# Two floors and two reciprocals of the quantised feed-forward taken together on two columns

## The reference, cut to what matters

```python
def _act_quant(x):
    scale = 127.0 / jnp.clip(jnp.max(jnp.abs(x), axis=-1, keepdims=True), 1e-05)
    xq = jnp.clip(jnp.round(x * scale), -128.0, 127.0) / scale
    return x + jax.lax.stop_gradient(xq - x)

def _bitlinear(x, w):
    return jnp.einsum('bsi,oi->bso', _act_quant(x), _weight_quant(w))
gate = jax.nn.silu(_bitlinear(x, w_gate))      # 256 -> 1024
up = _bitlinear(x, w_up)                       # 256 -> 1024
return _bitlinear(gate * up, w_down)           # 1024 -> 256
```

## Time and profile before

| | before |
|---|---|
| median of 3 runs | 1256.86 us (1255.3 to 1258.94) |
| the profiled execution | 1257.31 us, span of the core 1255.5 us |
| busy over the span | PE 94%, PEld 75%, DVE 65%, ACT 51%, POOL 45% |
| VectorE work of the feed-forward (first `am` to last `sc`) | 384.2 to 480.0 us of the span |
| small VectorE operations touched | 32 floors (TENSOR_SCALAR, 154 ns each) and 32 reciprocals (164 ns each) |
| wide ones beside them | `am` over 1024 values 1220 ns, `am` over 256 values 420 ns, 16 of each |
| granted TensorE clock | full in every slice of the span |

### The profile page before, as it was taken

One profiled execution on the slowest core, in us unless ns is written; L12 is line 12 of the kernel. 1 busy time (PEld: TensorE's weight loads), 2 busy tenths in 40 slices (PEclk: granted clock), 3 DMA queues, 4 the chain that ended last, 5 costly groups with the idle time before them and its releaser, 6 DMA issues.

```text
span 1255.5 us, 30244 instructions
## 1 busy us (share of the span) xinstructions
PE 1184.3 (94%) x9760; PEld 936.2 (75%) x9760; DVE 819.8 (65%) x1805; ACT 643.1 (51%) x1394; POOL 559.1 (45%) x833
## 2 busy tenths in 40 slices
PE   6899999989998878989998999999999999999998
PEld 4688888767775446767776888888888888888886
DVE  4688888867776888868999774444444544444444
ACT  4776677645454887535556434434343343433332
POOL 2244444657774444558885323333333233333232
PEclk9999999999999999999999999999999999999999
DMA  8200000000001001200000233333333333333331
GB/s 278 69 24 17 17 17 8 2 2 1 0 0 34 1 1 42 61 26 2 0 0 21 75 113 110 116 117 104 103 114 117 124 115 117 104 105 112 117 104 63
DMA packets 34041, 80.13 MB, mean 64 GB/s; under 512 B 4416, under 2 KB 12096, under 8 KB 33984
## 3 DMA queue, kind: packets, MB, share of 16 engines
q1 hardware_dynamic: 32800, 78.09, 19.1%
q10 hardware_dynamic: 1184, 1.31, 0.3%
HBM read 77.03 MB, written 2.36 MB: 63 GB/s over the span
## 4 chain that ended last, share of the span: by engine, by line
PE 78%; DVE 8%; issue 5%; POOL 4%; ACT 3%; DMA 0%; DVEq 0%; POOLq 0%; ACTq 0%; SPq 0%
PE ps L2443 10%; PE ps L2441 10%; PE ps L2442 10%; PE ps L444 5%; PE ps L2523 5%; PE ps L2524 5%; PE ps L2525 5%; PE ps L1095 4%; PE ps L459 3%; PE ps L432 3%; PE ps L1086 2%; PE ps L1074 2%; PE ps L1102 2%; PE ps L1065 2%; POOL Sm L1406 2%
## 5 line engine op out<-in xcount | busy, mean ns | idle before, releaser
L2810 POOL TENSOR_TENSOR sw<-sg,wb 128x512 f32<-128x512 f32 x136 | 176.4, 1297 | 386.7 <-ACT sg L2634 352.8
L2713 DVE TENSOR_TENSOR a<-sw,ps 128x512 f32<-128x512 f32 x136 | 93.4, 687 | 224.8 <-POOL sw L2810 224.5
L2639 ACT ACTIVATE ah<-a 128x512 fp32r<-128x512 f32 x136 | 86.0, 632 | 290.7 <-DVE a L2713 268.4
L2441 PE MATMUL ps<-Hh,wh 128*128 128x512 f32 x544 | 215.3, 396 | 0.0
L2442 PE MATMUL ps<-Hl,wh 128*128 128x512 f32 x544 | 214.4, 394 | 0.0
L2443 PE MATMUL ps<-Hh,wl 128*128 128x512 f32 x544 | 214.4, 394 | 0.0
L2717 DVE TENSOR_TENSOR al<-a,ah 128x512 fp32r<-128x512 f32 x136 | 95.6, 703 | 62.4 <-ACT ah L2639 59.3
L760 ACT ACTIVATE Pr<-ps,mx 128x256 f32<-128x256 f32 x256 | 104.1, 479 | 61.2 <-DVE mx L629 56.6
L2443 PEld LDWEIGHTS ps<-Hh,wl 128*128 128x128 f32 x544 | 101.8, 187 | 25.1
L2441 PEld LDWEIGHTS ps<-Hh,wh 128*128 128x128 f32 x544 | 101.9, 187 | 24.8 <-issue 0.8
L2442 PEld LDWEIGHTS ps<-Hl,wh 128*128 128x128 f32 x544 | 101.9, 187 | 23.5
(11 more groups left out here) (238 smaller groups left out, 2459.7 us busy)
## 6 DMA issues: line engine op xcount, KB each, us to landing
wb<-token_weights SPq DMA_DIRECT2D x64, 512.0 KB, 3.6
raw<-in_ew SPq DMA_DIRECT2D x66, 384.0 KB, 3.0
cT<-in_ctxT SPq DMA_DIRECT2D x16, 256.0 KB, 2.7
cx<-in_ctxT SPq DMA_DIRECT2D x15, 256.0 KB, 2.8
X<-in_x SPq DMA_DIRECT2D x1, 1536.0 KB, 7.1
wqkv<-in_wqkv SPq DMA_DIRECT2D x2, 768.0 KB, 5.1
raw3g<-in_wg SPq DMA_DIRECT2D x1, 1024.0 KB, 5.4
raw3u<-in_wu SPq DMA_DIRECT2D x1, 1024.0 KB, 7.6
```

Source lines behind the costliest of these rows:

```text
L2441: eng.matmul(ps[:, bank, :], wh[:, u, w], HhT[:, c, cols], start=(c == 0), stop=False)
L2713: eng.tensor_tensor(a[:, tt, :], sw[:, tt, :], ps[:, UB[tt], :], ALU.mult).then_inc(m_a, 1)
L2810: eng.tensor_tensor(sw[:, tt, :], sg[:, tt, :], wb[:, u, tt * UT:(tt + 1) * UT], ALU.mult).then_inc(m_sw, 1)
```

## The change

`am`, `ac` and `sc` get two columns for each buffer: column 0 for the inner values of tile i, column 1 for the row of tile i+2. Both maxima are taken first, and one floor and one reciprocal then work on both columns (`scale_both`). The two opening tiles have only column 1, and the last two steps only column 0. The readers take their column, and `round2` and `scale2` wait on the semaphores `f_sc` and `f_ac` of the joint operations (two of the semaphores go). `scale_both` carries the waits that protect both columns.

```diff
@@ -1492,8 +1492,8 @@
     L = 2
     base = NPAIR * L
 
-    am = sb("am3", [P, 2, 1]); ac = sb("ac3", [P, 2, 1]); sc = sb("sc3", [P, 2, 1]); dq = sb("dq3", [P, 2, 3])
-    am2 = sb("am32", [P, 2, 1]); ac2 = sb("ac32", [P, 2, 1]); sc2 = sb("sc32", [P, 2, 1]); dq2 = sb("dq32", [P, 2, 1])
+    am = sb("am3", [P, 2, 2]); ac = sb("ac3", [P, 2, 2]); sc = sb("sc3", [P, 2, 2])
+    dq = sb("dq3", [P, 2, 3]); dq2 = sb("dq32", [P, 2, 1])
     r = sb("r3", [P, 2, DIM]); xqT = sb("xqT3", [P, 2, HALF, P], BF16)
     sg = sb("sg3", [P, 2, INNER]); a = sb("a3", [P, 2, INNER]); ar = sb("ar3", [P, 2, INNER])
     aqT = sb("aqT3", [P, 2, 8, P], BF16); y = sb("y3", [P, 2, DIM])
@@ -1504,7 +1504,7 @@
     f_am = sem(n + "am"); f_ac = sem(n + "ac"); f_sc = sem(n + "sc"); f_dq = sem(n + "dq")
     f_r = sem(n + "r"); f_xt = sem(n + "xt"); f_xte = sem(n + "xte")
     f_g = sem(n + "g"); f_u = sem(n + "u"); f_sg = sem(n + "sg"); f_a = sem(n + "a")
-    f_am2 = sem(n + "am2"); f_ac2 = sem(n + "ac2"); f_sc2 = sem(n + "sc2"); f_dq2 = sem(n + "dq2")
+    f_am2 = sem(n + "am2"); f_dq2 = sem(n + "dq2")
     f_ar = sem(n + "ar"); f_at = sem(n + "at"); f_ate = sem(n + "ate"); f_o = sem(n + "o"); f_y = sem(n + "y")
     f_rnd = sem(n + "rnd")
     g["f_sg"] = f_sg; g["f_a"] = f_a; g["f_xte"] = f_xte; g["f_ate"] = f_ate; g["f_y"] = f_y
@@ -1628,16 +1628,30 @@
         eng.memset(rnd[:, 0:1], ROUND).then_inc(f_rnd, 1)
         eng.memset(rnd[:, 1:2], -ROUND).then_inc(f_rnd, 1)
 
-        def front1(i, u):
+        def row_max(i, u):
             eng.wait_ge(ln_h, base + i + 1)
-            eng.tensor_reduce(am[:, u, :], h[:, u, :], AX.X, ALU.max,
+            eng.tensor_reduce(am[:, u, 1:2], h[:, u, :], AX.X, ALU.max,
                               apply_absolute_value=True).then_inc(f_am, 1)
-            eng.wait_ge(f_am, i + 1)
-            reach(eng, f_dq, i - 1)
-
-            eng.tensor_scalar(ac[:, u, :], am[:, u, :], 1e-5, 1.0 / 127.0, ALU.max, ALU.mult).then_inc(f_ac, 1)
-            eng.wait_ge(f_ac, i + 1)
-            eng.reciprocal(sc[:, u, :], ac[:, u, :]).then_inc(f_sc, 1)
+
+        def inner_max(i, u):
+            eng.wait_ge(f_a, 2 * i + 2)
+            eng.tensor_reduce(am[:, u, 0:1], a[:, u, :], AX.X, ALU.max,
+                              apply_absolute_value=True).then_inc(f_am2, 1)
+
+        def scale_both(i, u):
+
+
+            c = slice(0 if within(i, 0, last) else 1, 2 if within(i, -2, last - 2) else 1)
+            if within(i, -2, last - 2):
+                eng.wait_ge(f_am, i + 3)
+            reach(eng, f_am2, i + 1)
+            reach(eng, f_dq, i + 1)
+            reach(eng, f_dq2, i - 1)
+            eng.tensor_scalar(ac[:, u, c], am[:, u, c], 1e-5, 1.0 / 127.0, ALU.max, ALU.mult).then_inc(f_ac, 1)
+            eng.wait_ge(f_ac, i + 3)
+            reach(eng, f_ar, i - 1)
+            reach(eng, f_r, i + 1)
+            eng.reciprocal(sc[:, u, c], ac[:, u, c]).then_inc(f_sc, 1)
 
         def mul(i, u, q):
             eng.wait_ge(f_sg, 2 * i + q + 1)
@@ -1648,22 +1662,12 @@
                                      scalar=dq[:, u, 1:2], in1=sg[:, u, q * 512:(q + 1) * 512],
                                      op0=ALU.mult, op1=ALU.mult).then_inc(f_a, 1)
 
-        def amax2(i, u):
-            eng.wait_ge(f_a, 2 * i + 2)
-            eng.tensor_reduce(am2[:, u, :], a[:, u, :], AX.X, ALU.max,
-                              apply_absolute_value=True).then_inc(f_am2, 1)
-            eng.wait_ge(f_am2, i + 1)
-            reach(eng, f_dq2, i - 1)
-            eng.tensor_scalar(ac2[:, u, :], am2[:, u, :], 1e-5, 1.0 / 127.0, ALU.max, ALU.mult).then_inc(f_ac2, 1)
-            eng.wait_ge(f_ac2, i + 1)
-            eng.reciprocal(sc2[:, u, :], ac2[:, u, :]).then_inc(f_sc2, 1)
-
         def body(i, u):
             v = 1 - u
             if within(i, 0, last):
                 mul(i, u, 0)
                 mul(i, u, 1)
-                amax2(i, u)
+                inner_max(i, u)
             if within(i, -1, last - 2):
                 reach(eng, f_r, i + 1)
                 ln_dve2(eng, L, i + 2, u, f_r)
@@ -1671,7 +1675,9 @@
                 eng.wait_ge(f_r, i + 1)
                 ln_dve2(eng, L + 1, 0, u, f_r)
             if within(i, -2, last - 2):
-                front1(i + 2, u)
+                row_max(i + 2, u)
+            if within(i, -2, last):
+                scale_both(i, u)
             if within(i, -2, last - 3):
                 ln_dve(eng, L, i + 3, v)
             elif isinstance(i, int) and i == last - 2:
@@ -1679,11 +1685,13 @@
 
         def first():
 
-            front1(0, 0)
+            row_max(0, 0)
+            scale_both(-2, 0)
             ln_dve(eng, L, 1, 1)
             yield PART
             ln_dve2(eng, L, 1, 1, f_r)
-            front1(1, 1)
+            row_max(1, 1)
+            scale_both(-1, 1)
             ln_dve(eng, L, 2, 0)
 
         yield from pairs(eng, body, first)
@@ -1700,10 +1708,10 @@
                            scale=dq[:, u, 0:1]).then_inc(f_sg, 1)
 
         def round2(i, u):
-            eng.wait_ge(f_sc2, i + 1)
+            eng.wait_ge(f_sc, i + 3)
             reach(eng, f_at, i - 1)
             eng.activation(ar[:, u, :], a[:, u, :], ACT.Identity, bias=rnd[:, 0:1],
-                           scale=sc2[:, u, :]).then_inc(f_ar, 1)
+                           scale=sc[:, u, 0:1]).then_inc(f_ar, 1)
 
         def xt_out(i, u):
             eng.wait_ge(f_xt, i + 1)
@@ -1758,18 +1766,18 @@
             eng.wait_ge(f_sc, i + 1)
             reach(eng, f_xt, i - 1)
             eng.nop(nofuse=True)
-            eng.tensor_scalar(r[:, u, :], h[:, u, :], sc[:, u, :], ROUND, ALU.mult, ALU.add).then_inc(f_r, 1)
+            eng.tensor_scalar(r[:, u, :], h[:, u, :], sc[:, u, 1:2], ROUND, ALU.mult, ALU.add).then_inc(f_r, 1)
 
         def scales(i, u):
             reach(eng, f_sg, 2 * (i - 1))
             reach(eng, f_a, 2 * (i - 1))
             eng.nop(nofuse=True)
-            eng.tensor_scalar(dq[:, u, :], wsc[:, :], ac[:, u, :], None, ALU.mult).then_inc(f_dq, 1)
+            eng.tensor_scalar(dq[:, u, :], wsc[:, :], ac[:, u, 1:2], None, ALU.mult).then_inc(f_dq, 1)
 
         def scale2(i, u):
-            eng.wait_ge(f_ac2, i + 1)
+            eng.wait_ge(f_ac, i + 3)
             reach(eng, f_y, i - 1)
-            eng.tensor_tensor(dq2[:, u, :], wsc[:, 2:3], ac2[:, u, :], ALU.mult).then_inc(f_dq2, 1)
+            eng.tensor_tensor(dq2[:, u, :], wsc[:, 2:3], ac[:, u, 0:1], ALU.mult).then_inc(f_dq2, 1)
 
         def add_x(t, u):
             eng.wait_ge(f_y, t + 1)
```

## The result

| | before | changed |
|---|---|---|
| median of 12 runs | 1256.72 us (1255.3 to 1258.94) | 1252.45 us (1251.83 to 1253.96) |
| profiled execution, span | 1255.5 us | 1251.2 us |
| VectorE instructions recorded | 1805 | 1777 |

The ratio is 0.9965 with a 95% interval of [0.9957, 0.9973]: 4.3 us, 0.35%, faster. The forecast was 1252.4 us.

What follows compares the result with a forecast made beforehand. VectorE was taken to bound the feed-forward loop at 5.34 us a tile; with ScalarE's 4.85 us taking over, 62.71 us becomes 58.06, 4.65 us earlier: 1252.7 us from the profiled 1257.31, stated as 1252.4 us median, range 1250.6 to 1256.2.

Steps and rivals of the forecast that it cites:

- VectorE sets the pace before: Feed-forward loop: VectorE bounds it at 5.34 us a tile, 10.67 us a turn, including 0.47 us idle at the turn back.
- Without the pair `h` starts 1.14 us after the wide maximum: VectorE: without floor and reciprocal before `h`, it starts after 1.14 us, not 1.67 and 1.53, saving 0.92 us a turn.
- ScalarE and TensorE then set the pace at 4.85 us a tile: Loop after the change: ScalarE with TensorE needs 3.72 + 1.13 = 4.85 us a tile and becomes the limit.
- the sum: From fourth to last `xqT`: ten steps at 4.85 and two at 4.78 make 58.06 instead of 62.71 us, 4.65 us earlier.
- VectorE's turn of 9.75 us, and a lead that loses at most 0.3 us: Loop: VectorE's turn falls from 10.67 to 9.75 us; it enters 0.8 us ahead and loses at most 0.3 us altogether.
- Rival B: VectorE's saving not had in full, or given back behind the layer: gain 0 to 3.5 us, 1255 us in the middle; chance 0.17.
- The second column costs under 0.01 us: Joint floor and reciprocal on VectorE: one column more in each was worth under 0.01 us, taken as nothing.
- The added waits cost nothing: VectorE: the joint floor's four semaphore waits and the joint reciprocal's three were taken as costing nothing.
- Rival C: Added waits worked off one by one behind the row's maximum: at 0.2 us each, 4.8 us slower, 1261.6 us; chance 0.06.
- rival A: TensorE's jump at the loop's turn back shows once `r` is early: gain only 3.1 us, 1254.0 us; chance 0.15.
- Both semaphores on the inner scale: Inner reciprocal moved later: would end at 435.70, just before `ar` at 435.72, with VectorE's 0.8 us lead on top; no cost.
- The gain passes to the end: Behind this layer everything waits in turn and DMA has 0% of the chain, so the whole 4.65 us reaches the end.

Runs made afterwards that it cites:

- 1: Kernel before with the wide maximum taken over 512 of the 1024 inner values: 1251.61 us, ratio 0.9956.
- 3: Kernel before with the five turns of the feed-forward's loop written out: 1251.03 us, ratio 0.9953.
- 2: Changed kernel with the wide maximum taken over 512 of the 1024 inner values: 1252.65 us, ratio 0.9955.
- 7: Changed kernel with four no-operation instructions on VectorE ahead of the feed-forward's first work: 1252.27 us, ratio 0.9965.
- 9: Changed kernel with two no-operation instructions ahead on VectorE: 1251.69 us in a single execution.
- 10: Changed kernel with one no-operation instruction ahead on VectorE: 1253.07 us in a single execution.
- 11: Changed kernel with three no-operation instructions ahead on VectorE: 1255.2 us in a single execution.
- Experiment 5: Changed kernel in its order, but floors and reciprocals as four separate one-column operations in steps 0 to 13: 1255.01 us, ratio 0.9979.
- 12: Kernel before with two no-operation instructions ahead on VectorE: 1258.28 us in a single execution.
- 4: Changed kernel with the feed-forward's loop written out: 1251.51 us, ratio 0.9954.
- 6: Changed kernel with ScalarE's rounding only 512 inner values wide from step 2 on: 1251.54 us, ratio 0.9960.

## Why the prediction was right, point by point

- *VectorE sets the pace before, and the loop's own cost is part of it.* Shown by 1 and 3: two quite different cuts into VectorE's time, neither of them the change, bring 4.85 and 4.91 us in the same stretch.
- *Without the pair `h` starts 1.14 us after the wide maximum.* 437.83 - 436.69 = 1.14 and 443.10 - 441.97 = 1.13. The reduction and reciprocal of the earlier trace rows were the right pattern.
- *ScalarE and TensorE then set the pace at 4.85 us a tile, the stretch takes 58.06 us.* Measured 4.83 and 58.09 us; the gain there is 4.62 us against 4.65 of the sum. That the cycle of ScalarE and TensorE is 4.83 us is shown by 2, where VectorE waits for it. That it sets the pace over all ten steps holds only as long as VectorE's lead does.
- *VectorE's turn of 9.75 us, and a lead that loses at most 0.3 us.* Both were mis-sized: the turn is 9.97 us, and VectorE loses 0.31 us in every turn. The two bodies save what the sum said, but where the loop turns back VectorE needs 440.52 - 439.66 = 0.86 us from the last statistics to `mul`, 0.66 before. This uses up the lead, and one step near the loop's end (450.51 to 455.60) takes 5.09 us instead of 4.83; the cost is 0.2 us in all. In experiments 7 and 9 to 11 it is 0.6 us (58.44 against 57.87): at the sixth `xqT` VectorE is some 0.60 us ahead there (its `mul` has started by so much before), 1.17 us in the two profiles of the changed kernel, in which the clock falls at 399 us and holds ScalarE back. That the fall makes the difference is read from these six traces and not tested.
- *Rival B.* Its cause did not come (`h` starts after 1.14 us), but its course did, by way of the turn back: a turn of 9.97 us, the lead gone after three or four turns and from there VectorE's pace. It cost 0.2 to 0.6 us and not the 1 us that B gave, since the loop has only five turns. In a longer loop VectorE would set the pace, at 4.99 us a tile; no run here has one.
- *The second column costs under 0.01 us.* A floor of two columns takes 0.17 us in the rows against 0.15, so the term is 0.02 us; on the reciprocal it is 0.01. It makes up 0.06 us of VectorE's turn.
- *The added waits cost nothing.* The joint floor starts 438.72, with the row's maximum over at 438.68. Rival C is out: in the two bodies that I read the floor and the reciprocal stand as close behind their source as before.
- *TensorE's jump is hidden.* 0.89 us across the turn back against 0.87 at the entry; rival A is out. The late step of 5.09 us lies where TensorE doesn't jump. The Trainium skill (Advanced Engine Details and Errata, Engine Queue Depths) gives TensorE a queue of 64 instructions; the 0.89 us agrees with a jump that is done while products still run, but no run here shows the queue's depth.
- *Both semaphores on the inner scale.* The joint reciprocal ended at 438.92 + 0.17 = 439.09 and `ar` started at 439.71, 0.57 us after `sg` began, as before; its row names nothing that it waited for. The move costs nothing, as said.
- *The gain passes to the end.* From the first VectorE work of the next layer to the end it is 1255.5 - 479.96 = 775.54 us before and 1251.2 - 476.01 = 775.19 changed: nothing is given back behind the layer.

What the prediction hadn't seen is where in the change the saving sits. It counted the pair that went as operations saved. Experiment 5 shows that more than half (2.60 of 4.62 us) comes from the place: the same pair costs 0.39 to 0.53 us between the wide maximum and `h`, and 0.27 us ahead of another small pair. The rows show where the difference sits: a dependent operation starts 0.03 us after the maximum has ended, an independent one 0.08 us before it ends.

That the forecast hit the median within 0.1 us is partly luck. Its own sum leads to 1256.86 - 4.65 = 1252.2 us; the 1252.4 us that it states does not follow from it. The 58.09 us of the stretch, too, are 58.44 in the traces without the fall of the clock, against 58.06 of the sum. In the two profiles the 4.3 us of the span are 4.62 us in the stretch, less 0.68 us by which the changed kernel enters it later (411.85 against 411.17), plus 0.35 us behind the layer. And the start of this layer differs by 2.9 us between all profiles (second `xqT` at 399.99 to 402.90), though all kernels do the same work up to it, but for the instructions put ahead.

## What to carry to other kernels

An operation between a long one and an independent one costs more than its own duration: 0.39 to 0.53 us for a pair of 0.15 and 0.16 us here, of which some two fifths (0.38 of 0.92 us a turn) go if the pair is only moved behind other small work. Before counting what a shorter engine saves, work out the cycle of the next one from the rows: here it stood 0.5 us a tile below. The change took 0.7 us a turn off VectorE and brought 4.6 us; another 1.1 us a turn on top of it brought 0.2 us. A comparison of two cycles isn't enough either: the longer one can stay hidden for the length of a short loop by the lead that its engine has on entering it. In a loop of short bodies the turn back of each engine belongs in the sum: hidden on TensorE, 0.66 or 0.86 us on VectorE.

## What the runs showed that I had not expected

- The turn back of the loop on VectorE, from the last statistics to `mul`, takes 0.66 or 0.67 us in the kernel before, with its half-width maximum, with two instructions ahead and in experiment 5, but 0.86 or 0.87 us in the changed kernel, with its half-width maximum and with one to four instructions ahead (from the third turn of the loop on). It goes with the loop's content and not with its place. What in the content does it stays open.
- Granted clock at the changes of layer (1.00 is the level of 2.4 GHz; a mean of 0.72 over a stretch means that part of it ran at 1.2): in the changed kernel (two profiles) and in experiment 2 it was low at 398 to 404 and 476 to 482 us; in the kernel before and experiments 5, 11 and 12 between 548 and 558 us, in 11 also at 396 to 398 us (0.51); and in 1, 3, 4, 6, 7, 9 and 10 at none of these. The slices of the page are 31 us long and their 9 stands for 90% and more, so falls as short as these don't show in it. The fall at 399 us is there when TensorE transposes weights and `r`, eight products in all, which run at half speed (1.06 us for the four of `wq` against 0.60); the step from the second `xqT` to the third is 5.90 - 5.66 = 0.24 us longer than in the kernel before. One instruction put ahead on VectorE takes both falls away, and with three one comes 2 us sooner, so they go with the exact timing and not with the change. That a kernel with none of them (experiment 7) has the same median says that they cost less than the spread of the runs.
